# Spills in rows of 512 tokens, x's last blocks kept on chip, the down product by chunks of channels: a Flamingo block on one core

## The chip, the cores and the metric

The kernel runs on one core of one Trainium2 chip. Its inputs and outputs lie in DRAM. The metric is the device time of one execution in microseconds; the kernel before takes 1567.4 us, the median of three executions.

## The reference

x is (4, 1024, 512), that is 4096 tokens of 512 channels; the context has 64 rows for each of the four batches. All is float32.

```python
x = x + tanh(g_xattn) * attention(layernorm(x), ctx, ctx)      # 16 heads of 64, mask k_pos <= q_pos
x = x + tanh(g_ffn) * ffn(layernorm(x))

def ffn(x):                       # hidden 512, inner 1536
    x = act_qdq(x)
    up = act_qdq(x @ lpbq_dequant(w_up).T)
    gate = act_qdq(x @ lpbq_dequant(w_gate).T)
    sig = fixed_qdq_u16(sigmoid(gate))       # multiples of 1/65536
    gate = act_qdq(gate * sig)
    o = act_qdq(gate * up)
    return o @ lpbq_dequant(w_down).T

def act_qdq(x):                   # 16 bit, one scale for the whole tensor
    scale = maximum(max(abs(x)) / 32767, 1e-12)
    return clip(round(x / scale), -32768, 32767) * scale
```

lpbq_dequant rounds the weights to 4 bits in blocks of 32. The scale of each act_qdq is a maximum over all 4096 tokens, so nothing can be rounded before the whole tensor has been seen. That cuts the ffn into stages: gate, up, a scan for the largest product, down.

## The kernel before

Each matrix operand is kept as a high and a low float32r part, and each product is three matmuls (high by high, high by low, low by high). A product of 128 inner channels with 512 tokens sums over four parts of the hidden channels: 12 matmuls of 128x512 (`product`, L1060). The tokens are taken in 8 blocks T of 512 (FT = 8), the inner channels in 12 groups `it` of 128 (IT = 12).

Work goes through five engines that each run their own list of instructions in the order in which it is written, and meet only at semaphores. SyncE (SP) issues all DMAs. A stage is a Block: at its end all engines wait for each other.

- **prepare, attend (L290, L455).** Weights and attention. The result x1 goes to DRAM, and xn, its layernorm. They aren't changed.
- **gate stage (L843).** TensorE transposes a block of xn (`transposes`, L1030), ScalarE and VectorE round it and split it into xh and xl (L954, L959, L985), and these 2 MB go to DRAM as x_d (L890). Then come 12 products; ScalarE evicts each from PSUM into one of four stage tiles (L972), VectorE takes its largest and smallest element (L994, L995), and SyncE writes it to `gate_d` (L897) as [tokens' quarter, inner channel, 128 tokens]: each partition writes four pieces of 128 floats (512 bytes). Beside it, jobs round the up and down weights. The loop transposes one block ahead, also in its last round, where the block isn't used. At the end, SyncE loads x's first block back (L935), and GpSimd spreads the gate's extremes over the partitions (`partition_all_reduce`, L1025), from which VectorE forms S_G and INV_G.
- **up stage (L1072).** 96 products in the order of T, from x blocks loaded into two pairs of buffers (L1128, each 2 MB in two DMAs), into four PSUM banks; ScalarE evicts (L1171) into three stage tiles, VectorE takes the largest magnitude (L1237), SyncE writes `up_d` (L1123), again in pieces of 512 bytes. Beside them, the gate's 32 tiles (128 tokens x 1536 channels, 768 KB) pass twice. First pass, T = 0 to 3, eight tiles a block, in slots after the evictions of it = 0, 1, 2, 4, 5, 6, 8, 9: SyncE loads tile k into one of three buffers gb (L1133) when tile k-3 is done, GpSimd rounds it to int16 (nq, L1146), ScalarE takes the sigmoid back into gb (L1159), VectorE turns it into an integer (mb, L1190) and forms the largest negative product with a custom pass (L1196), which writes into gb and so holds it. After block 3 comes the scale of the gated value (L1206 to L1218), with GpSimd's all-reduce (L1149). Second pass, T = 4 to 7: sigmoid again, from nq in SBUF, and the product back into nq (L1203).
- **scan (in down_phase, L1296).** For each of the 32 tiles, up is loaded again and rounded, and the largest |gated x up| is found. Of four tiles, three go through ScalarE, which takes both absolute values (L1334, L1335), and one custom pass of VectorE (L1358); the fourth through GpSimd (L1386) and two passes of VectorE (L1363, L1365). TensorE has nothing to do. An all-reduce on GpSimd (L1388) and six small steps give the last scales.
- **down stage (L1390).** For each tile g of 128 tokens: up is loaded and rounded (L1291), VectorE multiplies and rounds (`quantize`, L1461), ScalarE casts the high part (`high`, L1435), VectorE forms the low part (`low`, L1467), TensorE makes 36 matmuls into one of four banks, and VectorE scales and adds x1 (`finish`, L1454).

Of the kernel before, what the change touches and what calls it, by code (L numbers as in the profile page):

```python
# [15 lines left out]
F32 = mybir.dt.float32  # L16
# [9 lines left out]
P = 128  # L26
# [39 lines left out]
def flamingo_block(nc, x, ctx, g_xattn, g_ffn, w_q, w_k, w_v, w_o, w_gate, w_up, w_down, out):  # L66
# [22 lines left out]
    with ExitStack() as top:  # L89
# [54 lines left out]
        with ExitStack() as ff:  # L144
# [5 lines left out]
            ux, ux_in = [sb(ff, f"uxa{part}", [P, KT, 512], F32R) for part in ("h", "l")], sem("u_xa_in")  # L150
            load_w = [lambda eng, c, d=d, s=s: load_weights(eng, W, d, s, c) for d, s in zip(wsc, w_in)]
            gate_phase(mk, xn_d, x_d, ux, ux_in, gate_d, wsc, w_src, W, w_in[0], load_w, ident, S_X, INV_X,
                       (GPOS, GNEG, AP2, AN2, AMAX, S_G, INV_G))
            nq = sb(ff, "nq", [P, QT, I], I16)
            up_phase(mk, x_d, ux, ux_in, gate_d, up_d, W, w_in[1], load_w, nq, umx, fmx, sci, scu, S_X,
                     (S_G, INV_G, AP2, S_F2, C_F, S_U, INV_U), (T0, T1, T2, T3, T4))
            down_phase(mk, ux, up_d, x1_d, of, W, w_in[2], load_w[2], nq, pmx,
# [685 lines left out]
def gate_phase(mk, xn_d, x_d, ux, ux_in, gate_d, wsc, w_src, W, w_in, load_w, ident, S_X, INV_X, cols):  # L843
# [3 lines left out]
    GPOS, GNEG, AP2, AN2, AMAX, S_G, INV_G = cols  # L847
    with ExitStack() as ph:
        Wh, Wl = W
        xr = [sb(ph, f"xr{n}", [P, 4, H], F32) for n in range(2)]  # L850
        xq = [sb(ph, f"gxq{n}", [P, KT, 512], I16) for n in range(2)]
        xh = [sb(ph, f"gxh{n}", [P, KT, 512], F32R) for n in range(2)]
        xl = [sb(ph, f"gxl{n}", [P, KT, 512], F32R) for n in range(2)]
# [13 lines left out]
        red, all_, scl = sem("g_red"), sem("g_all"), sem("g_scl")  # L867
# [18 lines left out]
        def traffic(sp, i, last=False):  # L886
            for t in range(2):

                sp.wait_ge(*at(xl_done, 2 * KT * i, KT * t + KT))
                for part, dst in zip((xh[t], xl[t]), x_d):  # L890
                    sp.dma_start(dst[bass.ds(2 * i + t, 1), :, :].rearrange("a p k -> (a p) k"),
                                 part[:, :, :].bitcast(F32).rearrange("p k n -> p (k n)")).then_inc(x_out[t], 16)
                for it in range(IT):
# [3 lines left out]
                    sp.dma_start(gate_d[bass.ds(8 * i + 4 * t, 4), :, it * P:(it + 1) * P].rearrange("q p n -> p q n"),  # L897
                                 stage[n][:, :].rearrange("p (q n) -> p q n", q=4)).then_inc(st_out[n], 16)
# [19 lines left out]
        def _(sp):  # L918
# [14 lines left out]
            sp.wait_ge(*at(x_out[0], 0, 32 * FT // 2))  # L933
            for part, src in zip(ux, x_d):
                sp.dma_start(part[:, :, :].bitcast(F32).rearrange("p k n -> p (k n)"), src[0, :, :]).then_inc(ux_in, 16)  # L935
            for n in range(NS):
                sp.wait_ge(*at(st_out[n], 0, 16 * FT * IT // NS))
            for n in range(2):
                sp.wait_ge(*at(x_out[n], 0, 32 * FT // 2))
                sp.wait_ge(*at(xr_in[n], 0, 16 * (FT // 2 + (n == 0))))  # L940
# [5 lines left out]
        def _(act):  # L946
# [17 lines left out]
            with act.Fori(0, FT // 2) as i:  # L964
                for t in range(2):
                    for it in range(IT):
# [6 lines left out]
                        if it == 4:  # L973
                            parts(i, t + 1)
                        if it in range(5, 5 + KT):
                            high(i, t + 1, it - 5)
                        if it in (3, 7, 11):
                            job_hi(act, J, i, 3 * t + it // 4)

        @block.vector  # L980
        def _(dve):
# [7 lines left out]
            with dve.Fori(0, FT // 2) as i:  # L989
                for t in range(2):  # L990
                    for it in range(IT):
# [4 lines left out]
                        if it in range(6, 6 + KT):  # L996
                            low(i, t + 1, it - 6)
# [7 lines left out]

            dve.wait_ge(*at(g_pos, 0, FT * IT))
# [3 lines left out]
            dve.wait_ge(all_, 2)  # L1010
            dve.tensor_tensor(AMAX, AP2, AN2, ALU.max).then_inc(scl, 1)
            dve.wait_ge(scl, 1)
            dve.tensor_scalar(S_G, AMAX, 1.0 / QMAX, TINY, ALU.mult, ALU.max).then_inc(scl, 1)
            dve.wait_ge(scl, 2)
            dve.reciprocal(INV_G, S_G).then_inc(scl, 1)
            dve.wait_ge(scl, 3)

        @block.gpsimd
        def _(pool):
# [4 lines left out]
            pool.wait_ge(red, 2)  # L1024
            pool.partition_all_reduce(AP2, GPOS, P, RMAX).then_inc(all_, 1)  # L1025
            pool.partition_all_reduce(AN2, GNEG, P, RMAX).then_inc(all_, 1)

        @block.tensor
        def _(pe):
# [11 lines left out]
            transposes(0, 0)  # L1041
            with pe.Fori(0, FT // 2) as i:
                for t in range(2):
                    for it in range(IT):
# [9 lines left out]
                        if it == 3:  # L1054
                            transposes(i, t + 1)
                        if it % 4 == 3:
                            job_turn(pe, J, i, 3 * t + it // 4, ident)

# [13 lines left out]
def up_phase(mk, x_d, ux, ux_in, gate_d, up_d, W, w_in, load_w, nq, umx, fmx, sci, scu, S_X, cols, tmp):  # L1072
# [4 lines left out]
    S_G, INV_G, GMAX, S_F2, C_F, S_U, INV_U = cols  # L1077
    T0, T1, T2, T3, T4 = tmp
    with ExitStack() as ph:
        Wh, Wl = W  # L1080
        ux1 = [sb(ph, f"uxb{part}", [P, KT, 512], F32R) for part in ("h", "l")]
        x_pair = [ux, ux1]
# [5 lines left out]
        pU = [pb(ph, f"pU{n}") for n in range(4)]  # L1088
# [4 lines left out]
        x_in = [ux_in, sem("u_xb_in")]  # L1093
        u_ps, u_sb, u_max = sem("u_ps"), sem("u_sb", 4), sem("u_max")
        n_done, sig_done, m_done, f_done = sem("u_n"), sem("u_sig"), sem("u_m"), sem("u_f")
        link_s, red, all_, pos_n, pos_sig, pos_m, fmx_set, apart_v = (sem(f"u_{n}") for n in
            ("link", "red", "all", "pos_n", "pos_sig", "pos_m", "fmx_set", "apart_v"))
# [426 lines left out]
```

## Time and profile before

| | |
|---|---|
| median of three executions | 1567.4 us (1564.96 to 1568.44) |
| profiled execution | 1570.47 us, of it span 1568.7 |
| PE busy | 1345.2 us (86%) |
| DVE busy | 1096.6 us (70%) |
| ACT busy | 594.1 us (38%) |
| POOL busy | 235.2 us (15%) |
| DMA | 267.36 MB, mean 170 GB/s |
| granted TensorE clock, mean | 0.936 |

PE is TensorE (PEld its weight loads, which run beside), DVE VectorE, ACT ScalarE, POOL GpSimd, SP SyncE. L1067 is line 1067 of the kernel. A busy time is the time in which an engine executes; the span is the time from the first to the last instruction. The stages lie at about 590 to 883 us (gate), 896 to 1192 (up), 1196 to 1296 (scan) and 1302 to the end (down). PEclk is the TensorE clock that was granted, as a share of full speed.

### The profile page before, as it was taken

The numbers are of one execution on the slowest core, as the hardware profiler recorded it, in microseconds if no ns is written. First come the engines' busy times: TensorE is split into PE (matmuls) and PEld (weight loads), VectorE is DVE, ScalarE is ACT, GpSimd is POOL, SyncE is SP. The second block draws the span as 40 slices with busy tenths as digits, with TensorE's granted clock in tenths as the row PEclk, the third lists the DMA queues.
The fourth block names the chain that finished last, engine by engine and source line by source line (L and its number), as shares of the span: only waits on it lengthen the run. The fifth ranks groups of instructions, "written<-read, shape, count | busy, mean of one in ns | idle before, by whom it ended". The sixth has DMA issues, their size and how long they took to land. (4 is left out here: it accounts for less than half of the span.)

```text
span 1568.7 us, 19513 instructions
## 1 busy us (share of the span) xinstructions
PE 1345.2 (86%) x6152; PEld 1097.1 (70%) x6152; DVE 1096.6 (70%) x1440; ACT 594.1 (38%) x707; POOL 235.2 (15%) x254
## 2 busy tenths in 40 slices
PE   6589999999999958999999689889994008999999
PEld 5468778778778737888888567677883006888887
DVE  5558868868978735777767468878985995455553
ACT  2232232233232113333333344456656773333331
POOL 2102212212212210100100033440000220000000
PEclk9899999999999968999999899999997558999999
DMA  7701201201111139777777978885557874444442
GB/s 281 241 1 41 74 27 61 68 32 60 60 40 47 41 115 347 239 239 237 262 245 225 343 243 278 289 289 170 181 154 273 314 267 142 156 158 167 167 157 84
DMA packets 180679, 267.36 MB, mean 170 GB/s; under 512 B 10400, under 2 KB 120992, under 8 KB 176544
## 3 DMA queue, kind: packets, MB, share of 16 engines
q1 hardware_dynamic: 180352, 266.90, 50.6%
q8 instruction: 17, 0.28, 0.1%
q14 instruction: 22, 0.18, 0.0%
q10 hardware_dynamic: 288, 0.00, 0.0%
HBM read 155.71 MB, written 111.15 MB: 170 GB/s over the span
## 5 line engine op out<-in xcount | busy, mean ns | idle before, releaser
L1497 PE MATMUL pD<-Wh,doh 128*128 128x512 f32 x384 | 150.4, 392 | 109.5 <-DVE dol L1467 109.5
L1497 PEld LDWEIGHTS pD<-Wh,doh 128*128 128x128 f32 x384 | 72.6, 189 | 125.2 <-issue 109.9
L1067 PE MATMUL gpG<-gxh,Wh 128*128 128x512 f32 x384 | 153.2, 399 | 2.8 <-DVE gxl L985 2.0
L1067 PE MATMUL gpG<-gxh,Wl 128*128 128x512 f32 x384 | 150.8, 393 | 0.0
L1067 PE MATMUL gpG<-gxl,Wh 128*128 128x512 f32 x384 | 150.6, 392 | 0.0
L1497 PE MATMUL pD<-Wl,doh 128*128 128x512 f32 x384 | 150.1, 391 | 0.0
L1497 PE MATMUL pD<-Wh,dol 128*128 128x512 f32 x384 | 150.1, 391 | 0.0
L972 ACT ACTIVATE gst<-gpG,sc 128x512 f32<-128x512 f32 x96 | 66.4, 692 | 168.0 <-PE gpG L1067 168.0
L1159 ACT ACTIVATE gb<-nq,sc 128x1536 f32<-128x1536 int16 x64 | 100.8, 1575 | 63.4 <-POOL nq L1146 63.3
L790 PE MATMUL pO<-Vh,pTh 128*128 128x512 f32 x256 | 115.6, 451 | 10.2 <-DVE x L672 10.2
L994 DVE TENSOR_REDUCE gmx<-gst 128x512 f32 x96 | 65.8, 685 | 80.2 <-ACT gst L972 79.6
L1435 ACT ACTIVATE doh<-doq 128x1536 fp32r<-128x1536 int16 x32 | 47.7, 1490 | 168.4 <-PE pD L1497 157.0
L790 PE MATMUL pO<-Vh,pTl 128*128 128x512 f32 x256 | 102.4, 400 | 0.0
L790 PE MATMUL pO<-Vl,pTh 128*128 128x512 f32 x256 | 102.1, 399 | 0.0
L1454 DVE SCALAR_TENSOR_TENSOR dyo<-pD,sc,dxr 128x512 f32<-128x512 f32 x32 | 24.0, 750 | 108.0 <-PE pD L1497 108.0
L1067 PE MATMUL pU<-uxah,Wh 128*128 128x512 f32 x192 | 78.5, 409 | 23.9 <-DMA uxal<-xsl_d 12.4
L1171 ACT ACTIVATE ust<-pU,sc 128x512 f32<-128x512 f32 x96 | 64.6, 683 | 79.3 <-PE pU L1067 61.3
L1190 DVE TENSOR_SCALAR mb<-gb 128x1536 uint16<-128x1536 f32 x64 | 68.6, 1072 | 37.1 <-ACT gb L1159 37.1
L596 ACT ACTIVATE pTh<-pT 128x512 fp32r<-128x512 f32 x64 | 35.1, 596 | 140.4 <-PE pT L824 140.4
L1067 PE MATMUL pU<-uxbh,Wh 128*128 128x512 f32 x192 | 76.8, 400 | 10.2 <-ACT ust L1171 10.1
L1067 PEld LDWEIGHTS gpG<-gxh,Wh 128*128 128x128 f32 x384 | 72.8, 190 | 18.0 <-DVE gxl L985 2.4
L1067 PEld LDWEIGHTS gpG<-gxh,Wl 128*128 128x128 f32 x384 | 72.8, 190 | 15.7
(169 smaller groups left out, 3185.3 us busy)
## 6 DMA issues: line engine op xcount, KB each, us to landing
gate_d<-gst SPq DMA_DIRECT2D x96, 256.0 KB, 3.1
gb<-gate_d SPq DMA_DIRECT2D x32, 768.0 KB, 5.4
up_d<-ust SPq DMA_DIRECT2D x96, 256.0 KB, 3.8
uxah<-up_d SPq DMA_DIRECT2D x24, 768.0 KB, 4.5
uxal<-up_d SPq DMA_DIRECT2D x24, 768.0 KB, 5.1
xub<-up_d SPq DMA_DIRECT2D x16, 768.0 KB, 4.4
xr<-xn_d SPq DMA_DIRECT2D x9, 1024.0 KB, 6.4
xin<-in_x SPq DMA_DIRECT2D x32, 256.0 KB, 2.7
```

The lines of the kernel that those rows point to most:

```text
L596: act.activation(pTh[:, cs], pT[:, cs], ACT.Copy).then_inc(pTh_done, 1)
L790: mm = pe.matmul(pO[:, :], ps_[:, cs], vs[:, p, :], start=(p == 0 and ps_ is pTh and vs is Vh), stop=(p == PAIRS - 1 and ps_ is pTl))
L972: act.activation(stage[n][:, :], pG[m % 3][:, :], ACT.Copy, scale=S_X).then_inc(g_sb, 1)
L994: dve.tensor_reduce(gmx[:, 1, bass.ds(2 * IT * i + m, 1)], stage[m % NS][:, :], X, ALU.min).then_inc(g_neg, 1)
L1067: mm = pe.matmul(ps[:, :], Ws[:, it, kt * P:(kt + 1) * P], xs[:, kt, :], start=(kt == 0 and Ws is Wh and xs is xh), stop=(kt == KT - 1 and ...
L1159: act.activation(gb[k % NG][:, :], nq[:, k % QT, :], ACT.Sigmoid, scale=S_G).then_inc(sig_done, 1)
L1171: act.activation(stage[n][:, :], pU[it % 4][:, :], ACT.Copy, scale=S_X).then_inc(u_sb, 1)
L1190: dve.tensor_scalar(mb[k % NM][:, :], gb[k % NG][:, :], SIG_ONE, None, ALU.mult).then_inc(m_done, 1)
L1435: act.activation(oh[g % 2][:, :], oq[g % 2][:, :], ACT.Copy).then_inc(oh_done, 1)
L1454: dve.scalar_tensor_tensor(out=yo[n][:, :], in0=pD[g % 4][:, :], scalar=C_OUT, in1=xr[n][:, :], op0=ALU.mult, op1=ALU.add).then_inc(y_done, 1)
L1497: mm = pe.matmul(pD[g % 4][:, :], os_[:, cs], Ws[:, it, :], start=(it == 0 and os_ is oh[n] and Ws is Wh), stop=(it == IT - 1 and os_ is o ...
```

## The change

- **Spills.** `gate_d` and `up_d` keep the inner channel on the partitions and 512 tokens in a row: one piece of 2 KB a partition. A tile of 768 KB is now three channel groups of one block (a chunk), not 128 tokens with all channels; tile k of the passes is chunk k % 4 of a block.
- **Gate stage.** xh and xl live in buffers that outlast the stage (x_pair). The last two blocks aren't written to DRAM and stay there; the reload of block 0 goes, and so do the last round's unused transposes, casts and low parts. The scale of the gate isn't formed here.
- **Up stage.** The order of blocks is 6, 7, 0 to 5. x comes in pieces of 256 KB, two in each of the first four evictions of a block. There are six PSUM banks instead of four. A maximum is spread over partitions by a transpose of the column, repeated 128 times (`everywhere`), and a reduce from PSUM, where GpSimd's all-reduce stood; TensorE waits in its order for the column. A gate tile is rounded by GpSimd if its number is odd, and by ScalarE, one slot ahead of its sigmoid, if it is even. The custom pass writes into mb, and gb is free for the next load once the sigmoid is an integer (m_done). The scan's first two tiles are loaded in the last block.
- **Scan.** GpSimd does nothing. Six tiles in flight; of eight, five go by ScalarE's absolute values, three by two custom passes (scale -1, then 1).
- **Down stage.** TensorE takes a block of 512 tokens chunk by chunk, into four of eight banks; the last chunk finishes them one by one. The first chunk is prepared in thirds.

```diff
 gate_phase, traffic (SyncE)
+                if not last:
+                    sp.wait_ge(*at(xl_done, 2 * KT * i, KT * t + KT))
+                    for part, dst in zip((xh[t], xl[t]), x_d):
...
-                    sp.dma_start(gate_d[bass.ds(8 * i + 4 * t, 4), :, it * P:(it + 1) * P].rearrange("q p n -> p q n"),
-                                 stage[n][:, :].rearrange("p (q n) -> p q n", q=4)).then_inc(st_out[n], 16)
+                    dst = gate_d[bass.ds(8 * i + 4 * t + it // 3, 1), :, (it % 3) * 512:(it % 3 + 1) * 512]
+                    sp.dma_start(dst.rearrange("a p k -> (a p) k"), stage[n][:, :]).then_inc(st_out[n], 16)
...
-            sp.wait_ge(*at(x_out[0], 0, 32 * FT // 2))
-            for part, src in zip(ux, x_d):
-                sp.dma_start(part[:, :, :].bitcast(F32).rearrange("p k n -> p (k n)"), src[0, :, :]).then_inc(ux_in, 16)
 TensorE (ScalarE and VectorE alike)
-                        if it == 3:
+                        if it == 3 and not (last and t):
                             transposes(i, t + 1)
 up_phase
+def everywhere(pe, ps, column, ident):
+
+    return pe.transpose(ps, column.to_broadcast([P, P]), ident[:, :])
...
+        ORDER = [FT - 2, FT - 1, *range(FT - 2)]
...
+        def by_pool(k):
+            return k % 2 == 1
 SyncE
-                    sp.dma_start(up_d[4 * T:4 * T + 4, :, it * P:(it + 1) * P].rearrange("q p n -> p q n"),
-                                 stage[n][:, :].rearrange("p (q n) -> p q n", q=4)).then_inc(st_out[n], 16)
+                    sp.dma_start(up_d[4 * T + it // 3, :, (it % 3) * 512:(it % 3 + 1) * 512], stage[n][:, :]).then_inc(st_out[n], 16)
+                    if it < KT and 1 <= j < FT - 1:
+
+                        for part, src in zip(x_pair[(j + 1) % 2], x_d):
+                            sp.dma_start(part[:, it, :].bitcast(F32),
+                                         src[ORDER[j + 1], :, it * 512:(it + 1) * 512]).then_inc(xp_in[(j + 1) % 2], 16)
+                    for k in due[j, it]:
                         if k + NG < QT:
-                            sp.wait_ge(f_done, k + 1)
+                            sp.wait_ge(m_done, k + 1)
 ScalarE
+            def integer(k):
+
+                act.wait_ge(g_in[k % NG], 16 * (k // NG + 1))
+                act.activation(nq[:, k, :], gb[k % NG][:, :], ACT.Copy, scale=INV_G).then_inc(a_done, 1)
...
+                    for k in slot[j, it]:
+                        if k + 1 < QT and not by_pool(k + 1):
+                            integer(k + 1)
                         sigmoid(k)
 VectorE
-                dve.tensor_tensor_reduce(out=gb[k % NG][:, :], in0=nq[:, k, :], in1=mb[k % NM][:, :],
+                dve.tensor_tensor_reduce(out=mb[k % NM][:, :], in0=nq[:, k, :], in1=mb[k % NM][:, :],
...
+            dve.wait_ge(spread_s, 1)
+            link(dve.tensor_reduce(A2, pR[:, 0:2 * P].rearrange("p (a k) -> p a k", a=2), X, ALU.max))
+            link(dve.tensor_tensor(AMAX, A2[:, 0:1], A2[:, 1:2], ALU.max))
+            link(dve.tensor_scalar(S_G, AMAX, 1.0 / QMAX, TINY, ALU.mult, ALU.max))
+            link(dve.reciprocal(INV_G, S_G))
 TensorE
+                    if isinstance(i, int) and 2 * i + t == HT and it == 2:
+
+                        pe.wait_ge(red, 1)
+                        everywhere(pe, pR[:, 0:P], T0, ident).then_inc(spread_s, 1)
 down_phase, scan
+            ORDER = [*range(QT - 8, QT), *range(QT - 8)]
...
+            def by_act(k):
+                return k % 8 in (0, 2, 3, 5, 6)
 ScalarE
+                    act.activation(xui[k % NI][:, :], xub[k % NB], ACT.Abs if by_act(k) else ACT.Copy, scale=INV_U).then_inc(xui_done, 1)
+                    if by_act(k):
+                        if k >= NF:
+                            act.wait_ge(p_done, k - NF + 1)
+                        act.activation(fa[k % NF][:, :], nq[:, g, :], ACT.Abs).then_inc(fa_done, 1)
 VectorE
+                    if by_act(k):
+                        dve.wait_ge(fa_done, len([q for q in range(k + 1) if by_act(q)]))
+                        largest(dump, dump, u, 1.0, pmx[:, n:n + 1], p_done)
+                    else:
...
+                        largest(dump, nq[:, g, :], u, -1.0, pmx[:, 2:3], half_done)
+                        dve.wait_ge(half_done, halves)
+                        largest(dump, nq[:, g, :], u, 1.0, pmx[:, n:n + 1], p_done)
 down
+            def pieces(g):
+                return [(a * 512, (a + 1) * 512) for a in range(3)] if g == 0 else [(0, I)]
...
+                for s in range(QT + 4):
+                    if s + 2 < QT:
+                        quantize(s + 2)
+                    if s >= 4:
+                        finish(s - 4)
+                    if s + 2 < QT:
+                        low(s + 2)
 TensorE
+                        pe.wait_ge(*at(y_done, 8 * i, 4 * t - 4))
+                        for c in range(4):
+                            pe.wait_ge(w_in[c], 32)
+                            if c < 3:
+                                for a in range(3):
+                                    pe.wait_ge(*at(ol_done, 24 * i, 12 * t + 3 * c + a + 1))
+                                    mm = matmuls(t, c, a, range(4))
+                                mm.then_inc(d_ps, 1)
+                            else:
+
+                                pe.wait_ge(*at(ol_done, 24 * i, 12 * t + 12))
+                                for q in range(4):
+                                    for a in range(3):
+                                        mm = matmuls(t, c, a, [q])
+                                    mm.then_inc(d_ps, 1)
```

## Rows read from the trace of the kernel before

**Rows 1.** The busy time of stretches; columns: stretch, length, busy (x instructions), PEclk, DMA share, GB/s.

```profile
600.00:883.30 283.30, 280.19 (x1339) 233.41 (x1338) 198.80 (x357) 110.44 (x181) 24.19 (x23) 0.99 0.79 254
895.72:1064.00 168.28, 146.59 (x593) 115.93 (x594) 122.95 (x138) 78.82 (x80) 63.71 (x32) 0.95 0.82 277
1064.00:1192.46 128.46, 128.46 (x560) 105.84 (x558) 117.61 (x128) 79.64 (x80) 0.38 (x1) 0.99 0.60 184
```

**Rows 2.** The view of waits, 883 to 1303 us.

```profile
PE pU L1067 <- ACT ust L1171: 21.6, 11, 3.5
...
POOL nq L1146 <- DMA gb<-gate_d: 89.2, 29, 9.7
```

**Rows 3.** The timeline from gate stage to up stage; columns: start, length, instruction.

```profile
858.26 1.91 PE L1038 MATMUL gpX<-ident,xr 128*128 128x128 f32 x16
...
889.80 0.06 DVE L1220 MEMSET fmx<- 128x3 f32 x1 [1.56 <-PEq L848]
...
895.72 0.79 PE L1067 MATMUL pU<-uxah,Wh 128*128 128x512 f32 x1 [12.40 <-DMA uxal<-xsl_d]
```

**Rows 4.** The timeline of gate loads and their integers, up stage.

```profile
931.11 0.35 SPq L1133 DMA_DIRECT2D gb<-gate_d  x1
...
944.21 0.35 SPq L1133 DMA_DIRECT2D gb<-gate_d  x1
...
953.65 0.33 SPq L1133 DMA_DIRECT2D gb<-gate_d  x1
...
936.02 2.87 POOL L1146 TENSOR_SCALAR nq<-gb,sc 128x1536 int16<-128x1536 f32 x1 [6.55 <-DMA gb<-gate_d]
...
963.91 1.54 POOL L1146 TENSOR_SCALAR nq<-gb,sc 128x1536 int16<-128x1536 f32 x1 [8.00 <-DMA gb<-gate_d]
```

**Rows 5.** The groups by line, up stage; columns: busy us, mean ns, idle before.

```profile
L1159 ACT ACTIVATE gb<-nq,sc 128x1536 f32<-128x1536 int16 x64 | 100.8, 1575 | 63.4 <-POOL nq L1146 63.3
...
L1190 DVE TENSOR_SCALAR mb<-gb 128x1536 uint16<-128x1536 f32 x64 | 68.6, 1072 | 37.1 <-ACT gb L1159 37.1
L1171 ACT ACTIVATE ust<-pU,sc 128x512 f32<-128x512 f32 x96 | 64.6, 683 | 79.3 <-PE pU L1067 61.3 <-DMA up_d<-ust 11.9 <-issue 6.0
L1237 DVE TENSOR_REDUCE umx<-ust 128x1 f32<-128x512 f32 x96 | 64.6, 676 | 23.0 <-ACT ust L1171 23.0
L1196 DVE CUSTOM_DVE_ANT_0 gb<-nq,mb,fmx 128x1536 f32<-128x1536 int16 x32 | 64.0, 2001 | 0.0
```

**Rows 6.** Stretches with one kind of store.

```profile
1119.00:1122.00 3.00, 3.00 (x15) 2.49 (x14) 3.00 (x5) 2.38 (x3) 0.00 (x0) 1.00 0.31 87
1567.00:1568.00 1.00, 0.00 (x0) 0.00 (x0) 0.00 (x0) 0.00 (x0) 0.00 (x0) 1.00 0.70 262
```

**Rows 7.** The timeline of the scan.

```profile
1196.08 0.07 DVE L1350 MEMSET pmx<- 128x16 f32 x1 [0.97 <-PEq L1079]
...
1206.39 1.56 ACT L1334 ACTIVATE xui<-xub,sc 128x1536 int16<-128x1536 f32 x1
...
1209.23 1.56 ACT L1334 ACTIVATE dui<-uxah,sc 128x1536 int16<-128x1536 f32 x1
...
1244.31 3.09 DVE L1358 CUSTOM_DVE_ANT_0 xpp<-xga,dui,pmx 128x1536 f32<-128x1536 int16 x1
...
1247.33 1.81 DVE L1358 CUSTOM_DVE_ANT_0 xpp<-xga,xui,pmx 128x1536 f32<-128x1536 int16 x1
...
1249.07 1.75 DVE L1363 TENSOR_TENSOR xpp<-nq,xui 128x1536 f32<-128x1536 int16 x1
...
1250.96 1.75 DVE L1365 TENSOR_REDUCE pmx<-xpp 128x1536 f32 x1
...
1292.97 0.17 DVE L1368 TENSOR_REDUCE sc<-pmx 128x1 f32<-128x16 f32 x1
```

**Rows 8.** The chain that ended last.

```profile
1296.72 1.83 DVE doq L1461
...
1301.98 263.43 PE pD L1497 x1152
```

More of the change, by code:

```diff
@@ L963, in _, with evictions @@
                 high(0, 0, kt)
-            with act.Fori(0, FT // 2) as i:
+            def evictions(i, last=False):
                 for t in range(2):
@@ L972, in _ @@
                         act.activation(stage[n][:, :], pG[m % 3][:, :], ACT.Copy, scale=S_X).then_inc(g_sb, 1)
-                        if it == 4:
+                        if it == 4 and not (last and t):
                             parts(i, t + 1)
-                        if it in range(5, 5 + KT):
+                        if it in range(5, 5 + KT) and not (last and t):
                             high(i, t + 1, it - 5)
@@ L978, in _ @@
                             job_hi(act, J, i, 3 * t + it // 4)
+            with act.Fori(0, FT // 2 - 1) as i:
+                evictions(i)
+            evictions(FT // 2 - 1, last=True)
         @block.vector
@@ L988, in _, with extremes @@
                 low(0, 0, kt)
-            with dve.Fori(0, FT // 2) as i:
+            def extremes(i, last=False):
                 for t in range(2):
@@ L995, in _ @@
                         dve.tensor_reduce(gmx[:, 0, bass.ds(2 * IT * i + m, 1)], stage[m % NS][:, :], X, ALU.max).then_inc(g_pos, 1)
-                        if it in range(6, 6 + KT):
+                        if it in range(6, 6 + KT) and not (last and t):
                             low(i, t + 1, it - 6)
@@ L1004, in _ @@
                             job_lo(dve, J, i, q)
+            with dve.Fori(0, FT // 2 - 1) as i:
+                extremes(i)
+            extremes(FT // 2 - 1, last=True)
             dve.wait_ge(*at(g_pos, 0, FT * IT))
@@ L1039, in transposes, with gates @@
                     mm.then_inc(xT_ps, 1)
-            transposes(0, 0)
-            with pe.Fori(0, FT // 2) as i:
+            def gates(i, last=False):
                 for t in range(2):
@@ L1057, in _ @@
                             job_turn(pe, J, i, 3 * t + it // 4, ident)
+            transposes(0, 0)
+            with pe.Fori(0, FT // 2 - 1) as i:
+                gates(i)
+            gates(FT // 2 - 1, last=True)
 def product(pe, ps, Wh, Wl, xh, xl, it, ready):
@@ L1087, in up_phase @@
         mb = [sb(ph, f"mb{n}", [P, I], U16) for n in range(NM)]
-        pU = [pb(ph, f"pU{n}") for n in range(4)]
+        NU = 6
+        pU = [pb(ph, f"pU{n}") for n in range(NU)]
+        pR = pb(ph, "upR")
+        ORDER = [FT - 2, FT - 1, *range(FT - 2)]
         HT = FT // 2
@@ L1162, in _ @@
             act.activation(T3, sci[:, 0:1], ACT.Sigmoid, scale=S_G).then_inc(pos_sig, 1)
-            for T in range(FT):
+            if not by_pool(0):
+                integer(0)
+            for j in range(FT):
                 for it in range(IT):
-                    m = IT * T + it
+                    m = IT * j + it
                     n = m % NS
@@ L1293, in row_tile @@
[L1293 to L1308 removed]
+        ui_done = sem("d_ui")
@@ L1370, in _ @@
+                dve.wait_ge(p_done, QT)
+                dve.wait_ge(half_done, len([k for k in range(QT) if not by_act(k)]))
+                dve.tensor_reduce(T0, pmx[:, 0:3], X, ALU.max).then_inc(red, 1)
                 link(dve.tensor_tensor(T2, S_F2, S_U, ALU.mult))
+                dve.wait_ge(spread_s, 1)
+                link(dve.tensor_reduce(T1, pR[:, 0:P], X, ALU.max))
                 link(dve.tensor_tensor(T3, T1, T2, ALU.mult))
@@ L1388, in _ @@
[L1388 to L1408 removed]
+                head_starts(pool, [y_done])
@@ L1470, in _ @@
                 for g in range(2):
[L1471 to L1483 removed]
+                    quantize(g)
@@ new lines, in _ @@
+                with pe.Fori(0, FT // 2) as i:
+                    for t in range(2):
+                        pe.wait_ge(*at(y_done, 8 * i, 4 * t - 4))
[12 more added lines that the diff above has]
+                                    mm.then_inc(d_ps, 1)
```

426 lines of the change are left out of this document (193 added, 233 removed).

## The prediction

> **What bounds the kernel now.** I read the page first, then the busy time by stretches, then the waits, and last the timelines around the three places where TensorE stands still. The gate stage is TensorE's: 280.2 of 283.3 us busy [rows 1], so at most 3.1 us can be had there beside removed work. The second half of the up stage is its too, busy for all of 128.46 us. The down stage is one unbroken piece of 263.43 us, 1152 matmuls [rows 8]; that is 96 products of 12 matmuls at 2.74 us each, its slow start included. The up stage issues the same 96 products, but runs from 895.72 to 1192.46 us, 296.7 us: 33.3 more. All of it lies in the first half, where TensorE is busy for 146.6 of 168.3 us at a mean granted clock of 0.95 [rows 1]. There it waits 21.6 us in 11 pieces for evictions, while GpSimd waits 89.2 us for gate tiles from DRAM [rows 2]. Then there is a gap of 12.4 us ahead of the up stage [rows 3], and one from 1192.46 to 1301.98 us ahead of the down stage, 109.5 us, the scan [rows 7, 8]. So the change can earn in the two gaps and in the first half of the up stage.
>
> **Gate stage.** The last block's sixteen transposes of a block that nobody uses go: they take 1.91 us, of which some 0.2 lies over the next matmul [rows 3]. That is on TensorE's path: -1.7 us. Its casts (ScalarE, VectorE) and the last pair's two 2 MB stores go too, but a busy TensorE hides those, so 0; the bound is the 3.1 us above. SyncE's order is otherwise the same. If the unrolled last round cost instruction fetches, they would lie ahead of a full TensorE; I take 0.
>
> **Gap before the up stage.** Before, TensorE's last gate matmul ends at 883.3 and the first up matmul, 895.72, waits for the reload of x's first block [rows 3]. The other engines are in the new block at 889.8. After, x's last two blocks are in SBUF and are taken first; nothing but two 128x128 transposes stands ahead of the product, about 0.3 us. The start moves to 890.1: -5.6 us. The block's end still waits for the last weight store, so more than 6.5 isn't likely; if that store became the late one with its queue, 3. The gate scale (a reduce, three small VectorE steps) now runs beside the first product, which needs none of it; ScalarE's first eviction comes 5 us later (half clock), while the scale takes about 2. The GpSimd all-reduces go with no price.
>
> **Up stage, first half.** What was late: a ring of three gate buffers. A load issued at 931.11 reaches GpSimd at 936.02, 4.9 us; the same buffer's next load is issued at 944.21, so three tiles take 13.1 us and a block of eight 35, plus what the x loads add: behind their burst the load of 953.65 takes until 963.91, 10.3 us [rows 4]. Over four blocks that gives about 40 us each against 32.9 of products; 4 x 7 less the three spare PSUM banks (3 x 2.7 = 8) is 20, and the trace has 21.6 [rows 2], so I trust this way of counting.
>
> After, the buffer is free as soon as its sigmoid is an integer, without the reduce of 0.68 and the custom pass of 2.0 us [rows 5]. But even tiles are now rounded by ScalarE, and in its order that stands ahead of the sigmoid of the tile before. ScalarE waits there for a load that can be issued only after the tile two before that was finished. So the chain from one odd tile to the next is: integer of the sigmoid 1.1, SyncE and store issue 0.1, load 4.9 [rows 4], ScalarE's rounding 1.5 (not in the trace; the nearest forms of the same 1536 elements are 1.56 and 1.575, and back to back they cost 0.1 less [rows 5, 7]), sigmoid 1.5: 9.1 us for two tiles, where TensorE allows 8.2. Queued behind that wait are ScalarE's evictions, behind them SyncE's stores. x now comes in eight pieces of 256 KB over four evictions: 512 KB ahead of each of three gate loads, which costs two steps of the four in a block some 3.5 us together (1.4 to 1.6 us of transfer each time; bounds 0, if the slower pace spreads them, and 10.3 - 4.9 = 5.4 for one step, as behind the burst). Odd tile 1 to odd tile 29 are 14 steps: 3 in the first block (27), 11 in the next three (2.75 x 39.9 = 110), 137 in all. The second product ends near 898 (890.1, two products, 2.3 for the slow start); an eviction of 0.7, a rounding and a sigmoid bring tile 1's to 902, so tile 29's ends near 1039; tiles 30 and 31 need 5, and VectorE then 5.3 more to the reduce (1.1 + 0.7 + 2.0 + 2 x 0.7 [rows 5]): 1049. TensorE waits for exactly this reduce after its 51st product, in order, for the transpose that spreads the scale; without stalls it is there at 890.1 + 51 x 2.74 = 1030, and 1 more as the slow start lies all in front: 1031. Stall: 18 us. The six banks hide only how it is spread. After such a halt the clock is at its lower level: the first matmul of the stage shows 0.79 us [rows 3]. The mean of 0.95 over 168.3 us is 8 us lost in before's many halts and its start; I take 2.5 for the one (bounds 0 and 8). The stage: 263.4 + 18 + 2.5 = 283.9, so -12.8 us. Ends: stall 0 (-33) and stall 31 (0). GpSimd's half is off this chain: an odd tile is loaded three tiles ahead. The second half has VectorE at 117.6 of 128.5 us [rows 1], unchanged but for 2 us of scale steps: 0.
>
> **A rule beside it.** A 256 KB store in 512-byte pieces shows a DMA share of 0.31 at 87 GB/s, one in 2 KB pieces 0.70 at 262 [rows 6]: 281 against 374 GB/s at a full share, 0.2 us a store, 2.4 us of queue time a block. The Trainium skill, "DMA: Bandwidth & Descriptors", Specifications, puts the least size for line rate at 512 B, by which the new layout of the spills would give nothing; the stall would be an estimated 3 us longer and the time 1532. The rows speak against it.
>
> **The scan.** Before it lasts from 1196.08 to 1292.97, 96.9 us [rows 7]. Each fourth tile's GpSimd conversion falls on a VectorE pass and stretches it from 1.8 to 3.09 us [rows 7]; that goes. After, five tiles of eight take ScalarE 2.84 (two absolute values; 1206.39 to 1209.23) and VectorE 1.74 (1247.33 to 1249.07); three take ScalarE 1.5 and VectorE two passes, the second waiting for the first, 1.89 (1249.07 to 1250.96) + 1.74 [rows 7]. For eight: ScalarE 5 x 2.84 + 3 x 1.5 = 18.7, VectorE 5 x 1.74 + 3 x 3.65 = 19.65. VectorE sets it, 78.6 for 32 tiles. Ahead come the first two absolute values, 3.0, since two tiles are loaded already; the third tile's load, 4.9 after the start, makes one bubble of 1.5. 83.1 us: -13.8; the shorter last store lets it start 0.4 earlier. Ends: every pass at 1.89 (+5), or ScalarE without waits (-2). Loads need 768 KB in 2.5 us, with six buffers. In all -14.2.
>
> **From the scan to the first down matmul.** 1292.97 to 1301.98 is 9.0 us: all-reduce 2.0, six small steps 1.2, block change, then multiplying, rounding and subtracting a whole tile, 1.83 for the first of the three [rows 7, 8]. After: transpose and reduce 0.7 in the all-reduce's place, and the first chunk cut in three, so TensorE starts after the whole multiply and one third each of two passes, 2.7 in place of 5.3. 5.3 us: -3.7 (bounds -2 and -5).
>
> **Down stage.** The same 1152 matmuls. A chunk holds TensorE for 8.2 us; behind the buffer it frees stand ScalarE 1.5 and VectorE 1.8, and the finishing of an older tile 0.75 between, about 6. Cover 2 us; if it failed, 32 times a fraction of a us. I take 0, with +5 as the other end.
>
> **Sum.** -1.7 - 5.6 - 12.8 - 14.2 - 3.7 = -38.0. The profiled execution took 1570.5 us (span 1568.7), 3.1 over the median of 1567.4: 1532.5, or 1529 as a median.
>
> **Rivals.** (a) The gate ring no longer holds anything: if loads come in 4 us instead of 4.9, and x's pieces slip between, the step is 8.2, the stall and its clock go: 20 us less, 1509. For: less is written in small pieces, and GpSimd's waits go. Against: the DMA share of 0.82 [rows 1]. (b) The first half stays as slow as it was, since ScalarE's rounding puts back what the early release gives: stall 31, 1542. For: ScalarE waits in front of evictions, which nothing did before in that order. Against: 9.1 against 13.1 x 2/3 = 8.7 is nearly even, without x's burst. (c) Slower: the same ScalarE wait, with every load as slow as the one of 963.91 (10.3). A step is 14.5, 14 of them 203, 66 more: 1595. It decides where the step passes 12.5 us, that is a load over 8.3. For: four loads a block were that slow or nearly. Against: they were so behind a 2 MB burst, which is cut up. (d) The change doesn't do what it says in the scan: a VectorE pass with two SBUF inputs takes 3.09 for a reason other than GpSimd; 44 x 1.35 = 59 more, 1588. Against: at 1247.33 the same form takes 1.81.
>
> **How the numbers follow.** Forecast 0.50 (1518 to 1538 alone), (a) 0.15, (b) 0.26, (c) 0.06, (d) 0.03. The range takes (a) and (b) nearly whole: 1508 to 1552. Faster by over 0.2% (what a measurement can tell from no change) 0.89, within 0.2% 0.02, slower 0.09.
>
> **What would show it.** First up matmul near 888.5 us. In the up stage ScalarE's wait for gate tiles, in front of the rounding of even tiles, and one TensorE wait of some 15 us after the fifth block's third product: if it is missing, (a). First gate loads near 5 us; over 8, (c). Scan near 83 us with no VectorE pass over 1.9. A TensorE piece of about 263 us in the down stage; wrong if it is cut.

## The result, and the profile after

The changed kernel takes 1584.9 us (median of four, 1581.8 to 1589.4) against 1566.2 for the one before: a ratio of 1.0118, 95% interval 1.0097 to 1.0139. It is slower by 18.7 us, where I forecast 1529 with a range of 1508 to 1552, and gave slower 0.09. In the profiled execution of 1586.8 us (span 1585.0) the difference of the spans is 16.3 us, and every term that I forecast as a gain came out as one; the term that I put at 0 did not:

| term | predicted | in the trace |
|---|---|---|
| last transposes (gate stage from its first transposes to its last product) | -1.7 | 299.0 to 297.4: -1.65 |
| gap ahead of the up stage | -5.6 | 12.4 to 7.8: -4.6 |
| up stage | -12.8 | 296.7 to 293.5: -3.2 |
| from the last up matmul to the scan's last reduce | -14.2 | 100.5 to 88.7: -11.8 |
| from there to the first down matmul | -3.7 | 9.0 to 5.3: -3.7 |
| down stage | 0 | 263.4 to 303.9: **+40.5** |

(The rest is 1.2 us that the gate stage began later and small change at the end.) Busy time by stretches, the columns as in [rows 1], for the gate stage, the up stage up to TensorE's wait for the scale, the rest of it, and the down stage:

```profile
600.00:882.84 282.84, 278.30 (x1323) 231.65 (x1321) 196.23 (x353) 106.02 (x173) 24.22 (x23) 0.99 0.69 242
890.61:1059.00 168.39, 148.84 (x612) 119.71 (x612) 123.68 (x151) 101.70 (x99) 30.20 (x16) 0.95 0.82 276
1059.00:1184.07 125.07, 125.05 (x541) 103.01 (x541) 112.80 (x121) 77.96 (x77) 0.00 (x0) 0.98 0.59 192
1278.11:1582.00 303.89, 275.63 (x1152) 224.87 (x1152) 132.60 (x96) 92.99 (x62) 0.00 (x0) 0.94 0.38 130
```

The first three answer to [rows 1]; the last to the unbroken 263.43 us of [rows 8]: the same 1152 matmuls now lie in 303.9 us, 275.6 of them busy, at a mean clock of 0.94. Who waited, over the same time (total us, times, longest); the two lines on `pU` and `upR` answer to [rows 2]:

```profile
ACT dui L1328 <- DMA dub<-up_d: 110.4, 26, 5.2
DVE doq L1509 <- ACT dui L1328: 103.9, 26, 5.0
...
ACT nq L1166 <- DMA gb<-gate_d: 57.4, 15, 7.5
ACT xph L1483 <- PE pD L1537: 51.1, 14, 5.2
...
PE pD L1537 <- DVE dyo L1500: 28.0, 6, 6.7
...
PE pU L1065 <- ACT ust L1190: 14.1, 6, 4.8
...
PE upR L1072 <- DVE sc L1258: 5.4, 1, 5.4
```

In the down stage ScalarE waits 26 times for a load of up, 110 us in all, and VectorE 26 times for ScalarE. In the kernel before neither wait was there: ScalarE waited for TensorE (1302 to 1566 us of its trace):

```profile
ACT doh L1435 <- PE pD L1497: 157.0, 30, 6.0
```

TensorE's own waits, put down to VectorE's finish, are 28.0 us in 6. They lie at the head of the third and of each later block of 512 tokens, where TensorE waits for the finishing that frees its banks, and so meets the lateness of four chunks at once. The other 12 us of the 40.5 go with a stage whose granted clock is 0.94 and not 0.99.

The two places between stages, as in [rows 3, 7, 8]:

```profile
882.24 0.60 PE L247 MATMUL gjbank<-ident,gjd 128*128 128x128 f32 x4
...
889.29 0.66 PE L1072 MATMUL upR<-ident,sc 128*128 128x128 f32 x2 [6.45 <-PEq L847]
...
890.61 0.80 PE L1065 MATMUL pU<-xph,Wh 128*128 128x512 f32 x1 [0.66 <-POOLq L63]
...
1272.79 0.15 DVE L1409 TENSOR_REDUCE sc<-pmx 128x1 f32<-128x3 f32 x1
...
1275.38 2.08 DVE L1509 SCALAR_TENSOR_TENSOR doq<-nq,sc,dui 128x512 int16<-128x512 int16 x3 [0.53 <-PEq L1330]
...
1278.11 0.79 PE L1537 MATMUL pD<-Wh,xph 128*128 128x512 f32 x1 [4.63 <-DVE xpl L1516]
```

The second gap went as worked out: reduce at 1272.79, multiply in thirds at 1275.38, TensorE at 1278.11. In the first, the block starts at 889.25, half a microsecond before its time in [rows 3], and the matmul 1.4 after that: two transposes at the low clock (0.66 us, the granted clock 0.50), and 0.66 us of a wait for GpSimd's semaphore increments at the head of the stage, which before had been done long before x was there.

The scan's passes, and a stretch that holds only stores of the new layout (columns as in [rows 6]):

```profile
1228.39 1.81 DVE L1389 CUSTOM_DVE_ANT_0 xfa<-nq,xui,pmx 128x1536 int16<-128x1536 int16 x1
...
1230.39 1.82 DVE L1389 CUSTOM_DVE_ANT_0 xfa<-nq,xui,pmx 128x1536 int16<-128x1536 int16 x1 [0.19 <-DVE pmx L1389]
...
1232.14 1.81 DVE L1389 CUSTOM_DVE_ANT_0 xfa<-xfa,dui,pmx 128x1536 int16<-128x1536 int16 x1
...
1116.00:1119.00 3.00, 3.00 (x15) 2.49 (x14) 3.00 (x4) 0.87 (x2) 0.00 (x0) 1.00 0.23 87
```

From the first pass of a tile to its second it is 2.0 us (1228.39 to 1230.39), from the second to the next tile's 1.75; no pass exceeds 1.82. That is [rows 7] without the 3.09. The passes differ in two things from those before, GpSimd does nothing beside them and their output is int16 and not f32; no run tells the two apart. The stores show a share of 0.23 at 87 GB/s, 378 GB/s at a full share, against 281 in [rows 6].

### The profile page after: what moved, and what is told of

Its sections match the earlier page's. It is cut to its first block and busy times, and to the rows that moved or that the text cites. A ratio compares the mean times of both kernels' runs of the same rounds, so it can differ in the third digit from the quotient of the medians.

```text
span 1585.0 us, 18703 instructions
## 1 busy us (share of the span) xinstructions
PE 1354.6 (85%) x6141; PEld 1103.4 (70%) x6141; DVE 1091.5 (69%) x1468; ACT 620.7 (39%) x721; POOL 180.0 (11%) x225
## 5 line engine op out<-in xcount | busy, mean ns | idle before, releaser
L1537 PE MATMUL pD<-Wh,xph 128*128 128x512 f32 x384 | 155.7, 406 | 32.6 <-DVE dyo L1500 28.0
L1065 PE MATMUL pU<-xph,Wh 128*128 128x512 f32 x384 | 154.4, 402 | 14.9 <-ACT ust L1190 14.1
L1065 PE MATMUL gpG<-xph,Wh 128*128 128x512 f32 x384 | 152.5, 397 | 4.2 <-ACT gst L968 2.2
L1537 PE MATMUL pD<-Wl,xph 128*128 128x512 f32 x384 | 154.1, 401 | 0.0
L1537 PE MATMUL pD<-Wh,xpl 128*128 128x512 f32 x384 | 153.8, 401 | 0.0
L1065 PE MATMUL pU<-xpl,Wh 128*128 128x512 f32 x384 | 153.6, 400 | 0.0
L1065 PE MATMUL pU<-xph,Wl 128*128 128x512 f32 x384 | 153.1, 399 | 0.0
L1065 PE MATMUL gpG<-xph,Wl 128*128 128x512 f32 x384 | 150.1, 391 | 0.0
L1065 PE MATMUL gpG<-xpl,Wh 128*128 128x512 f32 x384 | 149.9, 390 | 0.0
L1537 PEld LDWEIGHTS pD<-Wh,xph 128*128 128x128 f32 x384 | 75.4, 196 | 51.3 <-issue 30.5
```

Source lines behind the costliest of these rows:

```text
L1065: mm = pe.matmul(ps[:, :], Ws[:, it, kt * P:(kt + 1) * P], xs[:, kt, :], start=(kt == 0 and Ws is Wh and xs is xh), stop=(kt == KT - 1 and ...
L1537: mm = pe.matmul(pD[4 * t + q][:, :], os_[n][:, cs], Ws[:, it, :], start=(it == 0 and os_ is oh and Ws is Wh), stop=(it == IT - 1 and os_ ...
```

## The experiments

**e1, the load ahead of the store.** Seven instructions of the down stage of the changed kernel, from the start of one rounding to the start of the next:

```profile
1343.91 1.58 ACT L1328 ACTIVATE dui<-dub,sc 128x1536 int16<-128x1536 f32 x1 [4.68 <-DMA dub<-up_d]
...
1345.52 1.82 DVE L1509 SCALAR_TENSOR_TENSOR doq<-nq,sc,dui 128x1536 int16<-128x1536 int16 x1 [4.43 <-ACT dui L1328]
1347.26 0.74 DVE L1500 SCALAR_TENSOR_TENSOR dyo<-pD,sc,xph 128x512 f32<-128x512 f32 x1
...
1348.03 0.34 SPq L1458 DMA_DIRECT2D out<-dyo  x1
...
1348.41 0.43 SPq L1454 DMA_DIRECT2D xph<-x_d  x1
...
1348.89 0.45 SPq L1323 DMA_DIRECT2D dub<-up_d  x1
...
1353.85 1.58 ACT L1328 ACTIVATE dui<-dub,sc 128x1536 int16<-128x1536 f32 x1 [4.93 <-DMA dub<-up_d]
```

Rounding 1.6, multiply, finish, then SyncE: the store of the output, the load of x1, and only then the load of the next chunk of up, which the next rounding waits for. Each releases the next; the loop takes 9.94 us (1343.91 to 1353.85), a chunk on TensorE 8.2. In the code, SyncE waits in `output(s - 4)` for a finish that VectorE does behind `quantize(s + 2)`, and the load of chunk s + 3 is in the queue behind that: a load waits for the multiply of the chunk just before it. The edit brings the load one step forward:

```diff
+                sp.wait_ge(ui_done, 1)
+                load_up(sp, 2)
                 for s in range(QT + 4):
-                    if s + 2 < QT:
-                        sp.wait_ge(ui_done, s + 1)
-                        load_up(sp, s + 2)
+                    if s + 3 < QT:
+                        sp.wait_ge(ui_done, s + 2)
+                        load_up(sp, s + 3)
                     if s >= 4:
                         output(s - 4)
```

> The changed kernel with one edit: in the down stage SyncE issues the load of up chunk s+3 ahead of the store of output s-4, not the load of chunk s+2 (one step further ahead). Theory (the load waits in SyncE's queue behind a store that waits for the multiply of the chunk loaded before, so load 4.8, rounding 1.6, multiply 1.7, finish 0.75 and three issues follow one another, 9.9 us a chunk): the down stage falls from 304 to 263 to 266 us and the whole from 1585 to about 1545 us. Rival (the order by chunks of channels itself makes TensorE wait, for buffers or banks): the down stage stays at 295 to 304, the whole at 1577 to 1585.

Measured: 1546.2 us (four runs, 1543.5 to 1547.9), 0.9873 of the kernel before (0.9854 to 0.9892), 38.7 us under the changed kernel. The same place in its trace:

```profile
1340.94 0.46 SPq L1323 DMA_DIRECT2D dub<-up_d  x1
...
1347.47 0.74 DVE L1502 SCALAR_TENSOR_TENSOR dyo<-pD,sc,xph 128x512 f32<-128x512 f32 x1
...
1348.24 0.34 SPq L1458 DMA_DIRECT2D out<-dyo  x1
...
1349.10 0.45 SPq L1323 DMA_DIRECT2D dub<-up_d  x1
...
1350.63 1.49 ACT L1485 ACTIVATE xph<-doq 128x1536 fp32r<-128x1536 int16 x1 [5.21 <-PE pD L1539]
...
1352.03 1.56 ACT L1328 ACTIVATE dui<-dub,sc 128x1536 int16<-128x1536 f32 x1
...
1353.90 1.81 DVE L1511 SCALAR_TENSOR_TENSOR doq<-nq,sc,dui 128x1536 int16<-128x1536 int16 x1
```

The load at 1340.94 is for the rounding of 1352.03, 11.1 us later, and ScalarE waits again for TensorE (the cast at 1350.63). TensorE's down stage runs in 263.1 us (1275.3 to 1538.4). So the place of the load in SyncE's order was the whole of the 40 us; with the load one step forward, the order by chunks of channels costs nothing that shows.

**e2, the same fault put into the kernel before.**

```diff
-                        load_up(sp, i, g + 3)
                         output(sp, i, g)
                         load_x(sp, i, g + 2)
+                        load_up(sp, i, g + 3)
```

> The kernel before with one edit: in the down stage SyncE issues the next up load behind the output's store and the x load, not ahead of them. Theory of the queue order: the same loop of load, rounding, multiply, finish now holds here too, with the order by tokens untouched: 32 tiles at 9.5 to 10 us instead of 8.2, down stage 295 to 315 us, whole 1600 to 1620. Rival (the order by chunks is the cause): no change, 1567.

Measured: 1618.8 us (one run), 51.9 over the kernel before; TensorE's down stage is 314.3 us for 263.4. The order by tokens is untouched here, and the loop is the same, 10.16 us from rounding to rounding:

```profile
1398.57 1.58 ACT L1291 ACTIVATE dui<-uxal,sc 128x1536 int16<-128x1536 f32 x1 [5.02 <-DMA uxal<-up_d]
...
1400.39 1.82 DVE L1461 SCALAR_TENSOR_TENSOR doq<-nq,sc,dui 128x1536 int16<-128x1536 int16 x1 [5.05 <-ACT dui L1291]
...
1402.12 0.74 DVE L1454 SCALAR_TENSOR_TENSOR dyo<-pD,sc,dxr 128x512 f32<-128x512 f32 x1
...
1404.17 0.33 SPq L1285 DMA_DIRECT2D uxah<-up_d  x1
...
1408.73 1.58 ACT L1291 ACTIVATE dui<-uxah,sc 128x1536 int16<-128x1536 f32 x1 [5.00 <-DMA uxah<-up_d]
```

So the fault needs no part of the new down stage. What matters is the distance. In the kernel before, `load_up(g + 3)` stands behind `output(g - 1)`, whose finish VectorE does behind the multiply of tile g + 1, two tiles back. In the changed kernel `load_up(s + 2)` stands behind `output(s - 5)`, and so behind the multiply of chunk s + 1, one chunk back. e2 makes the two one; e1 makes the one two again.

**e3, all gate tiles by GpSimd.** ScalarE's roundings of even tiles in the changed kernel's up stage; in brackets how long ScalarE stood before each, and for what:

```profile
939.01 1.58 ACT L1166 ACTIVATE nq<-gb,sc 128x1536 int16<-128x1536 f32 x1 [4.51 <-DMA gb<-gate_d]
...
952.76 1.58 ACT L1166 ACTIVATE nq<-gb,sc 128x1536 int16<-128x1536 f32 x1 [7.51 <-DMA gb<-gate_d]
...
961.14 1.58 ACT L1166 ACTIVATE nq<-gb,sc 128x1536 int16<-128x1536 f32 x1 [2.72 <-DMA gb<-gate_d]
...
970.27 1.58 ACT L1166 ACTIVATE nq<-gb,sc 128x1536 int16<-128x1536 f32 x1 [2.90 <-DMA gb<-gate_d]
...
981.36 1.58 ACT L1166 ACTIVATE nq<-gb,sc 128x1536 int16<-128x1536 f32 x1 [4.28 <-DMA gb<-gate_d]
...
995.06 1.57 ACT L1166 ACTIVATE nq<-gb,sc 128x1536 int16<-128x1536 f32 x1 [7.46 <-DMA gb<-gate_d]
```

One block is 42.3 us (939.01 to 981.36), and 42.3 again to the next like it (952.76 to 995.06), for four steps of 8.4 to 13.8. The edit, on e1:

```diff
         def by_pool(k):
-            return k % 2 == 1
+            return True
```

> e1_load_first with all 32 gate tiles rounded by GpSimd, none by ScalarE. Theory (in the up stage ScalarE waits in front of evictions for even tiles; two tiles need about 10.6 us where TensorE gives 8.2): the wait of ScalarE for gate loads goes, the ring of three takes 10 to 11 us for three tiles, under TensorE's pace, TensorE's 19.5 us of waits fall to under 6 and the up stage from 293.5 to 265 to 272 us; whole 22 to 28 us under e1_load_first. Rival (the DMA engines, 0.82 of the time busy, set the pace of the first half): the up stage stays within 5 us of 293.

Measured: 1526.3 us (1523.1 to 1530.9), 0.9735 of the kernel before (0.9713 to 0.9758), 19.9 under e1. The up stage goes from 291.1 us (e1) to 279.7, 8 to 15 us more than I had expected (265 to 272), and TensorE's waits in it (e3's lines, then e5's below in the same form) from 21 to under 10:

```profile
PE pU L1065 <- ACT ust L1190: 5.5, 2, 2.9
PE upR L1072 <- DVE sc L1258: 4.3, 1, 4.3
```

The mechanism is shown, its size was put too high: TensorE's waits fell by 11 us, the up stage by 11.4, where I had let nearly all of e1's 21 us go. The rival, that the DMA engines set the pace, had the stage stay within 5 us of 293. The other 8 us of the 19.9 aren't in the up stage; the profiled executions are e1's fastest and e3's slowest and differ by 12.5 only, so a part is scatter between executions.

**e4, spills in pieces of 512 bytes again.**

```diff
-                    sp.dma_start(up_d[4 * T + it // 3, :, (it % 3) * 512:(it % 3 + 1) * 512], stage[n][:, :]).then_inc(st_out[n], 16)
+                    dst = up_d[4 * T + it // 3, :, :].rearrange("p (q c n) -> p q c n", q=4, c=3)
+                    sp.dma_start(dst[:, :, it % 3, :], stage[n][:, :].rearrange("p (q n) -> p q n", q=4)).then_inc(st_out[n], 16)
```

and the same for `gate_d`; the down stage takes its columns from the new places.

> e1_load_first with both spills written in pieces of 512 bytes again (a tile's columns in the order token quarter, channel group, token), all else the same but the first down chunk, which waits for all its thirds (+1.3 us). Theory (a 2 KB piece saves DMA time: 378 against 281 GB/s at a full share): a block's stores cost 2.4 us of queue more, two to three blocks in the chain: the up stage 5 to 12 us longer than e1_load_first. Rival (512 bytes are enough for the full rate): within 2 us of it.

Measured: 1551.5 us (1550.6 to 1555.7), 0.9901 (0.9882 to 0.992), 5.3 over e1, of which 1.2 are the whole first chunk's. The up stage is 301.4 us in the profile against 291.1, but the profiled executions are 12.2 apart where the medians are 5.3, so the 10.3 is an upper reading; by the medians some 4 are left for the pieces. That is more than the rival's 2 and less than the 5 to 12 of the theory, and the intervals of e1 and e4 overlap a little, though every execution of e4 was slower than every one of e1. Stores alone in its trace:

```profile
1119.00:1122.00 3.00, 3.00 (x15) 2.47 (x14) 3.00 (x4) 2.44 (x3) 0.00 (x0) 1.00 0.30 87
```

The share is 0.30 at 87 GB/s, 290 GB/s at a full share, where 2 KB pieces give 378. By the Trainium skill, "DMA: Bandwidth & Descriptors", Specifications, 512 B is the least size for line rate; here the fourfold piece is 1.3 times as fast, and the measurement decides.

**e5, the maximum asked for later.** On e3: TensorE waits for the gated value's maximum behind the fifth product, not the third, and VectorE takes the scale's steps and the second pass from there.

```diff
-            first = 3 if j == HT else 0
+            first = 5 if j == HT else 0
...
-                    if (j, it) == (HT, 3):
+                    if (j, it) == (HT, 5):
                         scale_of_f()
...
-                    if isinstance(i, int) and 2 * i + t == HT and it == 2:
+                    if isinstance(i, int) and 2 * i + t == HT and it == 4:
```

> e3_all_pool with the spread of the gated value's maximum two products later in TensorE's order (after the fifth, not the third, product of the fifth block), and the second pass's slots from there. Theory (TensorE's wait of 4.3 us for that reduce is the queue order again, and the halt costs clock behind it): the wait falls under 1 us, the up stage from 279.7 to 272 to 276 us, whole 4 to 8 us under e3_all_pool. Rival (the halt only comes later, since VectorE is late anyway and now has less room for the second pass): no change or up to 3 us longer.

Measured: 1521.3 us (1517.7 to 1522.4), 0.9705 (0.9685 to 0.9725), 5.0 under e3, and no execution as slow as e3's fastest; the up stage is about 272 us, as the theory had it, and the wait for the maximum 0.2 us.

```profile
PE pU L1065 <- ACT ust L1190: 4.4, 2, 3.4
...
PE upR L1072 <- DVE sc L1258: 0.2, 1, 0.2
```

**e6, x in a burst.** On e3, x by two transfers of 1 MB after a block's first eviction, as before the change. The counts of x's semaphore, changed to match, aren't shown.

```diff
-                    if it < KT and 1 <= j < FT - 1:
+                    if it == 0 and 1 <= j < FT - 1:
...
-                            sp.dma_start(part[:, it, :].bitcast(F32),
-                                         src[ORDER[j + 1], :, it * 512:(it + 1) * 512]).then_inc(xp_in[(j + 1) % 2], 16)
+                            sp.dma_start(part[:, :, :].bitcast(F32).rearrange("p k n -> p (k n)"),
+                                         src[ORDER[j + 1], :, :]).then_inc(xp_in[(j + 1) % 2], 16)
```

> e3_all_pool with x loaded as in the kernel before, 2 MB in two transfers after a block's first eviction, not in eight pieces over four evictions. Theory (one gate load in each block then stands behind the burst and takes some 10 us, not 6, in a ring that has 3 to 4 us to spare a block): up stage 279.7 to 282 to 290 us. Rival (the bytes are the same, and the pieces delay three loads a little where the burst delays one): within 2 us, or shorter.

Measured: 1522.8 us (1520.9 to 1524.9), 0.972 (0.9702 to 0.9738), 3.5 under e3, with runs and an interval that overlap e3's. The up stage is 272.7 us in the profile, where my theory had 282 to 290: it is refuted, and whether the burst is faster this pair doesn't show by itself. DMA issues of the gate tiles (count, KB each, median us to landing), e3:

```profile
gb<-gate_d SPq DMA_DIRECT2D x29, 768.0 KB, 6.9
```

and e6:

```profile
gb<-gate_d SPq DMA_DIRECT2D x29, 768.0 KB, 5.3
```

The median load is 1.6 us shorter with the burst. I took this for the reason of a gain, and tested it with e9.

**e7, no x.** On e1: x's loads in the up stage and TensorE's waits for them are left out; the products use what is in the buffers.

```diff
-                    if it < KT and 1 <= j < FT - 1:
...
-                if not isinstance(i, int) or i:
-                    pe.wait_ge(*at(xp_in[t], 16 * 2 * KT * i, 0))
```

> e1_load_first without x's loads in the up stage: it leaves out reading blocks 0 to 5, and the products use the blocks that are there. It prices what the pieces of x cost in ScalarE's chain of even tiles, where I had 3.5 us a block and the trace has steps of 11.3 and 13.7 us among steps of 9. Theory (they cost 6.5 to 7 us a block): every step 8.5 to 9.3 us, TensorE's waits in the up stage from 21 to 3 to 9 us, the up stage from 291 to 270 to 280. Rival (the long steps come from the four evictions and the distance of the slots, not from x): steps of 11 and 13 us stay, the up stage over 285.

Measured: 1535.8 us (1530.0 to 1539.2), 0.9799 (0.9769 to 0.983), 10.4 under e1. Up stage 283.5 us, TensorE's waits:

```profile
PE pU L1065 <- ACT ust L1185: 9.9, 5, 4.3
...
PE upR L1072 <- DVE sc L1253: 3.1, 1, 3.1
```

Neither theory held its numbers. ScalarE's 14 steps from tile 2 to tile 30 take 144.2 us in e1 and 135.6 here, so x costs the chain 8.6 us, 3.1 a block: my 3.5 was about right. It was the plain step that was too short: 9.7 us on average without any x, and single ones of 10.6, where I had 9.1.

**e9, the burst with ScalarE's rounding kept** (e1 with the edit of e6).

> e1_load_first with x in two transfers of 1 MB after a block's first eviction, ScalarE's rounding of even tiles kept. If the eight pieces slow every gate load (median 6.9 us in e3 against 5.3 in e6), the steps of ScalarE's chain shorten here too: 14 steps from 144 to 136 to 141 us and the whole 3 to 8 us under e1_load_first. If instead the chain is hit by the burst (one load of 10 us a block, as my prediction had it), the whole is 3 to 10 us longer than e1_load_first.

Measured: 1542.0 us (1541.2 to 1543.7), 0.9845 (0.9817 to 0.9873), 4.2 under e1, with an interval that overlaps that of e1; 14 steps in 142.1 us. The direction of e6 again, but its reason isn't: the median gate load, first e1, then e9,

```profile
gb<-gate_d SPq DMA_DIRECT2D x29, 768.0 KB, 5.6
```

```profile
gb<-gate_d SPq DMA_DIRECT2D x29, 768.0 KB, 6.2
```

is longer with the burst here. The other expectation, 3 to 10 us longer, is refuted as well. e8, below, against e5 is a third pair, 6.9 us apart in the same direction. All three point one way, and none is clear of its intervals. Why the burst is no worse, and seems some us better, stays open.

**e8, the version the runs point to:** e1, e3, e5 and e6 together.

> The version that the runs so far point to: e3_all_pool with both the later spread of the gated value's maximum (e5) and x in two transfers of 1 MB (e6). If the two gains (5.0 and 3.5 us) have causes of their own they add up: about 1518 us. If the second only removes lateness that the first hides as well: 1520 to 1522, no better than either alone.

Measured: 1514.4 us (five executions, 1513.2 to 1520.7), 0.9677 of the kernel before (0.9649 to 0.9705). That is 11.9 under e3, no less than the 8.5 of e5 and e6 by themselves, so they don't hide one another; the 3.4 more are within the scatter of the three. The up stage is 265.5 us for products that need 263; what is left of TensorE's waits there is one:

```profile
PE upR L1072 <- DVE sc L1258: 1.8, 1, 1.8
```

It beats both kernels, by 52.8 us and by 70.5.

## Why the prediction was wrong

- **The step that failed is the down stage's.** I wrote: "A chunk holds TensorE for 8.2 us; behind the buffer it frees stand ScalarE 1.5 and VectorE 1.8, and the finishing of an older tile 0.75 between, about 6." That follows a buffer from TensorE back to TensorE. It leaves out the other loop, through SyncE: load 4.8, rounding 1.6, multiply 1.7, finish 0.75, and about 1 of issues, 9.9 us. e1 takes the loop away and the 40 us with it; e2 puts it into the kernel before and adds 52. The prediction doesn't follow SyncE's queue in the down stage at all. My other end of +5 was no bound: a loop that is longer than TensorE's chunk costs its excess every time. Here it binds from the first finish on: the multiplies that start at 1316.35 and 1563.18 are 25 steps apart, 9.87 us each, 1.7 over TensorE's 8.2, together 42 us.
- **None of the four rivals was this one.** (c) and (d), the slower ones, lie in the up stage and in the scan. In the scan (d) is refuted: no pass over 1.82 us. With this step put right the rest was still too low: e1 takes 1546.2 us, inside the range, 17 over the forecast.
- **Up stage, the mechanism right, the size off.** The wait of ScalarE for even tiles, 57.4 us in 15 pieces, is there, and TensorE's waits of 14.1 and 5.4 us make 19.5, where I had 18. But I let them be one halt at the scale, with 2.5 us of low clock behind it; they were seven, and the stage's 293.5 us are 12.9 above 261.1 (96 products at 2.72) and these waits, where I had 4.8 for start and halt together. So the gain was 3.2 us and not 12.8, in time nearer to rival (b), which had none. The sign I had named for (a), that no wait of some 15 us stands at the scale, came up (it was 5.4) without (a) being so: most of TensorE's waiting was for evictions. The sum of the steps was 144 us, not 137; by e7 that is the plain step's, 9.7 for 9.1. What rival (a) had, a first half without such waits, came only with e3, e5 and e6. One thing I gave no price: in the kernel before, GpSimd's first rounding starts at 908.69 us, 21 us behind its all-reduce with no releaser in the trace, in the changed kernel at 895.56. That lateness may be a part of what was slow before; no run isolates it.
- **Scan.** 84.8 us from the block's start to the last reduce, for 83.1: the step to a second pass takes 2.0 us, not 1.89, and there are twelve. The block starts 3.9 us behind the last up matmul, where I had 3.2 (3.6 before, less 0.4). (1.89 + 1.74 is 3.63 and not 3.65, 0.2 us over the scan.)
- **Gate stage, gap, tail:** right to 0.1, 1.0 and under 0.1 us. The microsecond is the transposes at the low clock and GpSimd's increments. The 0.1 of the gate stage is luck in part: its first products ran at the high clock sooner (first matmuls of 0.50 and 0.40 us, before 0.79 and 0.63), a gain of 1.3 us that I didn't have, and TensorE waited 2.2 us for an eviction where it had waited 0.7.
- **The rule on 512 bytes** had the new layout give nothing. The stores' shares went by the row, and the whole by some 4 us between e1 and e4 beside the first chunk.

## What to carry to other kernels

For each load that a stage issues, walk the loop in which it is: who waits for it, who waits for that, and whether one of them is a wait that stands ahead of the same load in its queue. The distance in steps between a load and the wait in front of it matters as much as its place, and a loop longer than the bottleneck's step costs the excess every time. An early release earns little if another engine takes its work in an order that waits for the load sooner: the changed kernel's up stage gained 3.2 us with ScalarE's roundings, and 11.4 more when they went (e3).

## What I had not expected of the hardware

A store of 256 KB in pieces of 2 KB takes a DMA share of 0.23 at 87 GB/s, in pieces of 512 bytes 0.30: 378 against 290 GB/s at a full share. Several short halts of TensorE cost more than their length: in the changed kernel's down stage 28 us of shown waits go with 40.5 us of time, at a mean granted clock of 0.94, between the levels of 1.2 and 2.4 GHz, where the unbroken stage has 0.99. In e2 39 us of waits in 26 pieces go with 51 of time, there at a mean clock of 0.98, so the clock isn't all of it. And x in eight pieces of 256 KB seems slower than in two of 1 MB (e3 against e6, 3.5 us; e1 against e9, 4.2; e5 against e8, 6.9), each time with overlapping intervals, and the length of the gate loads doesn't explain it.
